# A quantised feed-forward matmul: plain tiles against Strassen's seven block products

## What is computed

```python
def _dequant(weight_q, scale, zp):          # weight_q (2048, 2048) int32, scale and zp (2048, 64)
    q = weight_q.astype(jnp.float32).reshape(N, num_groups, gs)
    return ((q - zp[:, :, None]) * scale[:, :, None]).reshape(N, K)
w = _dequant(weight_q, scale, zp)
out = jnp.einsum('bsk,nk->bsn', x, w) + bias       # x (2, 1024, 2048)
x = x + _L0_ffn_ref(_layernorm(x, axis=-1), ...)   # the layer's input is added back
```

## Time and profile before

| | |
|---|---|
| three timed runs | 2302.66, 2303.94, 2315.09 us (median 2303.94) |
| the profiled execution: time, span | 2315.36 us, 2313.6 us |
| PE busy | 2196.6 us, 95% of the span, 11560 matmuls |
| DVE, ACT, POOL busy | 57%, 46%, 43% |
| moved by DMA | 424.6 MB, mean 184 GB/s |
| granted TensorE clock, mean | 0.97 |
| gated products | about 950 to 1310 us |
| feed-forward: first and last matmul | 1598.4 and 2310.1 us |

### The profile page before, as it was taken

One profiled execution on the slowest core, in us unless ns is written; L12 is line 12 of the kernel. 1 busy time (PEld: TensorE's weight loads), 2 busy tenths in 40 slices (PEclk: granted clock), 3 DMA queues, 4 the chain that ended last, 5 costly groups with the idle time before them and its releaser, 6 DMA issues.

```text
span 2313.6 us, 34024 instructions
## 1 busy us (share of the span) xinstructions
PE 2196.6 (95%) x11560; PEld 1802.5 (78%) x11560; DVE 1325.6 (57%) x1734; ACT 1065.9 (46%) x1596; POOL 995.5 (43%) x621
## 2 busy tenths in 40 slices
PE   6898989999988999899999999998999999999999
PEld 4777766666657888788788889997778888888887
DVE  6777766777746888423332357677564364374222
ACT  3444448888875777521321356666322122122111
POOL 0111138999997677200000187873353253153110
PEclk8999989999997999899999999999999999999999
DMA  5678763333335665445453568779665565565443
GB/s 183 205 229 264 235 185 87 97 102 96 105 86 172 218 216 219 157 131 177 144 175 121 189 224 317 295 291 334 226 207 176 163 212 168 160 209 176 152 137 100
DMA packets 208916, 424.60 MB, mean 184 GB/s; under 512 B 16482, under 2 KB 132194, under 8 KB 181940
## 3 DMA queue, kind: packets, MB, share of 16 engines
q1 hardware_dynamic: 208820, 423.31, 56.2%
HBM read 284.31 MB, written 138.67 MB: 183 GB/s over the span
## 4 chain that ended last, share of the span: by engine, by line
PE 72%; DMA 9%; DVE 8%; ACT 4%; issue 4%; POOL 2%; SPq 2%; DVEq 0%; ACTq 0%; POOLq 0%
PE s_psF L2695 9%; PE s_psF L2696 9%; PE s_psF L2697 9%; PE s_m_psG L2317 7%; PE s_m_psU L2317 7%; PE s_psO L922 4%; PE s_w_psA L1901 4%; PE s_w_psB L1901 4%; DMA s_q_xc<-xP 4%; PE s_psS L868 4%; PE s_psX L899 3%; PE s_w_psR L1406 2%; DMA s_f_q<-wq 2%; DVE s_a_mx L948 1%; PE s_w_psT L1933 1%
## 5 line engine op out<-in xcount | busy, mean ns | idle before, releaser
L2695 PE MATMUL s_psF<-s_f_wh,s_f_xh 128*128 128x512 f32 x1024 | 400.2, 391 | 9.7 <-DVE s_f_xl L2573 5.0
L2697 PE MATMUL s_psF<-s_f_wh,s_f_xl 128*128 128x512 f32 x1024 | 399.1, 390 | 0.0
L1053 POOL TENSOR_TENSOR s_a_pl<-s_a_pf,s_a_ph 128x1024 fp32r<-128x1024 f32 x128 | 302.0, 2393 | 21.8 <-ACT s_a_pf L1010 21.7
L2569 ACT ACTIVATE s_f_xh<-s_f_xl 128x2048 fp32r<-128x2048 f32 x64 | 122.7, 1917 | 359.0 <-PE s_psF L2697 326.0
L2668 POOL TENSOR_TENSOR s_f_xb<-s_f_xb,s_f_fb 128x512 f32<-128x512 f32 x64 | 93.2, 1456 | 341.6 <-DMA s_f_xb<-x 324.7
L2069 POOL TENSOR_TENSOR s_w_yl<-s_w_y,s_w_yh 128x1024 fp32r<-128x1024 f32 x32 | 76.0, 2399 | 370.0 <-ACT s_w_yh L1981 370.0
L948 DVE TENSOR_REDUCE s_a_mx<-s_psS 128x1 f32<-128x512 f32 (+2 forms) x248 | 179.2, 754 | 97.0 <-PE s_psS L876 96.7
L2695 PEld LDWEIGHTS s_psF<-s_f_wh,s_f_xh 128*128 128x128 f32 x1024 | 192.7, 188 | 52.8 <-DVE s_f_xl L2573 6.7
L2697 PEld LDWEIGHTS s_psF<-s_f_wh,s_f_xl 128*128 128x128 f32 x1024 | 192.6, 188 | 40.1
L2696 PE MATMUL s_psF<-s_f_wl,s_f_xh 128*128 128x512 f32 x512 | 200.0, 391 | 0.0
L2573 DVE TENSOR_TENSOR s_f_xl<-s_f_xl,s_f_xh 128x2048 fp32r<-128x2048 f32 x64 | 160.0, 2501 | 48.5 <-ACT s_f_xh L2569 48.5
(11 more groups left out here) (316 smaller groups left out, 5633.8 us busy)
## 6 DMA issues: line engine op xcount, KB each, us to landing
s_f_xl<-xnT SPq DMA_DIRECT2D x64, 1024.0 KB, 5.8
s_q_xt<-xT SPq DMA_DIRECT2D x16, 1024.0 KB, 7.7
s_q_xc<-xP SPq DMA_DIRECT2D x16, 1024.0 KB, 9.8
hsD<-s_q_hs SPq DMA_DIRECT2D x16, 1024.0 KB, 4.9
s_w_hin<-hsD SPq DMA_DIRECT2D x16, 1024.0 KB, 5.0
hs<-s_w_res SPq DMA_DIRECT2D x16, 1024.0 KB, 3.9
s_m_raw<-giT SPq DMA_DIRECT2D x32, 512.0 KB, 4.8
mlpT<-s_m_mo SPq DMA_DIRECT2D x64, 256.0 KB, 2.4
```

Source lines behind the costliest of these rows:

```text
L1053: pool.tensor_tensor(pl[:, r, cols], pf[:, j - 1], ph[:, r, cols], ALU.subtract).then_inc(pl_ok, 1)
L2695: pe.matmul(out[:], xh[:, u % 2, kt], high(c, kt), start=(kt == 0), stop=False)
L2697: mm = pe.matmul(out[:], xl[u % 3][:, kt], high(c, kt), start=False, stop=(kt == KD - 1))
```

## The change

**The product.** Rows are cut into two halves (tiles 0 to 7, 8 to 15), the inner dimension into two, and each pair of column blocks (a group, GROUPS = 2) into its two blocks. The 2x2 by 2x2 block product is then done with seven products in place of eight; each product's factors are sums or differences of one or two blocks, and its result is added to, or subtracted from, one or two of the four blocks of the output. The table PRODUCTS lists for each product its row terms, its weight terms and its targets:

**SP's order.** Per unit u: wait for `finish(u)`, store what is complete, load the rows of unit u+4 (one or two terms), load pieces of the next product's weights (one or two terms), load a base where one is due:

```diff
+            for u in range(SEAM, UNITS):
+                sp.wait_ge(y_ok, adds[u + 1])
+                for cell in touched(u):
+                    if last_unit[cell] == u:
+                        store(sp, cell)
+                if u + 4 < UNITS:
+                    load_x(sp, u + 4)
+                    load_second(sp, u + 4)
+                for n in pieces(u):
+                    load_piece(sp, n)
```

**DVE's order** is `finish(u-1)`, `lo_x(u+2)`, then the low parts of the pieces that SP loaded at unit u-2; POOL's is `add_second(u+2)`, `add_piece` of those pieces, bias of a base:

```diff
         def vector(dve):
-            for u in range(3, UNITS):
-                for v in made_in(u):
-                    less_zero(dve, v)
-                finish(dve, u)
+            for u in range(SEAM, UNITS):
+                if u > SEAM:
+                    finish(dve, u - 1)
                 if u + 2 < UNITS:
                     lo_x(dve, u + 2)
-                for v in made_in(u):
-                    lo_piece(dve, v)
+                for n in pieces(u - 2):
+                    lo_piece(dve, n)
```

**The weights** are no longer made in the feed-forward. All four blocks are made in the gated products, 16 portions of 1 MB in place of 4, and eight differences of halves (`p_diff`, stored as `wD`) for the first product of each group:

```diff
-        made = (11, 18, 35, 42)
+        made = tuple(range(4, 4 + 3 * C * KH, 3))
...
+                if u - 5 in made:
+                    plane["difference"](dve, made.index(u - 5))
```

More of the change, by code:

```diff
@@ L2051, in body @@
                     normalise(s, p)
+                    if not live(1):
+                        between(s.off - TILES if s.reg is None else None)
                     evacuate(s, 0)
@@ new lines, in store, with product, touched @@
+            sp.dma_start(dst, w[:, i % RING]).then_inc(w_out, 16)
+            if second(i):
+                sp.wait_ge(diff_ok, pairs(i) + 1)
+                dst = io["wD"][i // (2 * KH)].rearrange("p (r j n) -> p r j n", j=KH, r=KH // 2)[:, :, i % KH]
+                sp.dma_start(dst, diff[:]).then_inc(d_out, 16)
+        return dict(load=load, less_zero=less_zero, times_scale=times_scale, difference=difference, store=store,
+                    w_out=w_out, d_out=d_out, groups=C * KH)
+def build_ffn(nc, io, k, zone, w2):
+    PAIRS = TILES // 2
+    HK = KD // 2
+    GROUPS = C // 2
+    PRODUCTS = (
[7 more added lines that the diff above has]
+    )
+    STEPS = len(PRODUCTS)
+    UNITS = GROUPS * STEPS * PAIRS
+    SEAM = PAIRS
+    ISSUE = (0, 0, 1, 2, 3, 4, 5, 6)
+    def product(u):
+        return PRODUCTS[u // PAIRS % STEPS]
+    def touched(u):
+        return [(u // (STEPS * PAIRS), half, n, u % PAIRS) for half, n, _ in product(u)[3]]
+    adds, last_add, first_add, last_unit = [0], {}, set(), {}
+    for u in range(UNITS):
+        adds.append(adds[-1] + len(product(u)[3]))
+        for cell in touched(u):
+            last_unit[cell] = u
+    two = [0]
+    for u in range(UNITS):
+        two.append(two[-1] + (len(product(u)[1]) == 2))
+    made = [0]
+    for n in range(UNITS):
+        made.append(made[-1] + (len(product(n)[2]) == 2))
+    summed_x = [u for u in range(UNITS) if two[u + 1] > two[u]]
+    summed_w = [n for n in range(UNITS) if made[n + 1] > made[n]]
+    stores = {}
+    for u in range(UNITS):
+        for cell in touched(u):
+            if last_unit[cell] == u:
+                stores[cell] = len(stores)
+    base_at = {}
+    for j in range(PAIRS):
+        base_at[0, 0, 1, j] = base_at[0, 1, 1, j] = j - 2 * PAIRS
+        base_at[0, 0, 0, j] = j + 4
+        base_at[0, 1, 0, j] = j + 14
+        for half, n in ((0, 1), (1, 0), (0, 0), (1, 1)):
+            base_at[1, half, n, j] = last_unit[0, half, n, j] + (4 if (half, n) == (0, 1) else 2)
+    bases = sorted(base_at, key=lambda cell: (base_at[cell], cell[1]))
+    base_of = {cell: b for b, cell in enumerate(bases)}
+    RB, RY, RW = 8, 4, 5
@@ new lines, in build_ffn, with acc, high, low @@
+        mm_ok, b_ok, y_ok, fb_in = (sem(n) for n in ("mm_ok", "b_ok", "y_ok", "fb_in"))
+        def acc(cell):
+            return home[cell[1:]]
+        def high(q, kt):
+            if q % 2:
+                return wh1[:, kt]
+            return whA[:, kt] if kt < 2 else whB[:, kt - 2]
+        def low(q, kt):
+            if q % 2:
+                return wl1[:, kt]
+            return wlA[:, kt] if kt < 2 else wlB[:, kt - 2]
+        def rows(u, term):
+            half, part, _ = term
+            return io["xnT"][u % PAIRS + PAIRS * half][:, part * HK * P:(part + 1) * HK * P]
@@ new lines, in weights, with load_second @@
+        def weights(q, term, kt):
+            part, n, _ = term
+            at = (part * HK + kt) * H
+            return io["wF"][q // STEPS * 2 + n][:, at:at + H]
+        def load_x(sp, u):
+            if u >= 4:
+                sp.wait_ge(mm_ok, u - 3)
+            sp.dma_start(xl[u % 4][:].bitcast(F32).rearrange("p t j -> p (t j)"), rows(u, product(u)[1][0])).then_inc(x_in[u % 4], 16)
+        def load_second(sp, u):
+            if len(product(u)[1]) == 2:
+                i = two[u]
+                if i >= 3:
+                    sp.wait_ge(x_lo, summed_x[i - 3] + 1)
+                sp.dma_start(xs[i % 3][:].rearrange("p t j -> p (t j)"), rows(u, product(u)[1][1])).then_inc(xs_in[i % 3], 16)
@@ new lines, in store, with pieces @@
+        def store(sp, cell):
+            g, half, n, j = cell
+            i, tile, c = stores[cell], half * PAIRS + j, 2 * g + n
+            if i >= RY:
+                sp.wait_ge(y_out[i % RY], 16 * (i // RY))
+            sp.dma_start(io["y"][tile * P:(tile + 1) * P, c * H:(c + 1) * H], acc(cell)[:]).then_inc(y_out[i % RY], 16)
+        def pieces(u):
+            q, m = (u + 1) // PAIRS + 1, (u + 1) % PAIRS
+            if q >= GROUPS * STEPS:
+                return ()
+            return tuple(q * HK + kt for kt in range(HK) if ISSUE[kt] == m)
@@ L2604, in times_scale @@
[L2604 to L2614 removed]
+            load_x(sp, 11)
+            load_second(sp, 11)
@@ new lines, in sync, with whole_x, whole_w @@
+            for r in range(RY):
+                sp.wait_ge(y_out[r], 16 * len(stores) // RY)
+        def whole_x(u):
+            return xs[two[u] % 3][:] if len(product(u)[1]) == 2 else xl[u % 4][:].bitcast(F32)
+        def whole_w(n):
+            if made[n + 1] > made[n]:
+                return ws[:, made[n] % 4]
+            return low(n // HK, n % HK).bitcast(F32)
+        def hi_x(act, u):
+            if len(product(u)[1]) == 2:
+                act.wait_ge(x_sum, two[u] + 1)
+            else:
+                act.wait_ge(x_in[u % 4], 16 * (u // 4 + 1))
+            if u >= 3:
+                act.wait_ge(mm_ok, u - 2)
+            act.activation(xh[u % 3][:], whole_x(u), ACT.Copy).then_inc(x_hi, 1)
```

471 lines of the change are left out of this document (273 added, 198 removed).

## The result

The changed kernel takes **2406.1 us** (median of 4 runs, 2404.8 to 2409.9). Beside it the kernel before took 2309.5 us, a ratio of **1.042** (95% interval 1.038 to 1.046): 4.2% slower, where the forecast was 0.7% faster and its range ended at 2338. The profiled execution spans 2404.4 us, 90.8 more than that of before.

What follows compares the result with a forecast made beforehand. The prediction took the feed-forward as bound by PE's number of matmuls. Its terms, -87 - 5 + 59 + 12 + 5 = -16 us, put the median of 2303.9 us at 2288 us, 0.7% faster, range 2240 to 2338.

Steps and rivals of the forecast that it cites:

- Step 1: Feed-forward on PE: 3072 matmuls become 2688 at an unchanged 0.2267 us each, -87.0 us.
- Step 2: Feed-forward: PE's waits where weights are made from integer pieces go away, -5 us.
- Step 3: Feed-forward: the loop through SP's loads takes 6.27 us per unit against PE's 5.44, +59 us including turns.
- Rival B: Feed-forward loop is longer, rows landing in 6.7 us: term +106, 2335 us in all; chance 0.28.
- turns of POOL and DVE over the bias: Feed-forward, first group: a bias add standing between costs 0.6 us per unit in some 25 units, 15 us.
- Step 4: Gated products: added weight portions cost only where rows and second-half weights load together, +12 us (+2 to +25).
- Rival C: Gated products: 3 MB bursts delay rows in all chunks, costing 45 us instead of 12, 2321 us; chance 0.10.
- Step 5: Joint before the feed-forward: earlier first pieces give -4, late rows and lost slack cost more, +5 us (-4 to +15).
- Rival A: Feed-forward: the loop does not bind, turns alone do, costing 16 us; 2245 us in all; chance 0.22.

Runs made afterwards that it cites:

- a1_order: Changed kernel with the feed-forward's loads of rows and weight pieces issued before SP's wait for the additions: 2312.7 us, 1.002 of the kernel before.
- p1_plane: Kernel before with all sixteen weight portions and eight differences made in the gated products, its feed-forward untouched: 2352.2 us, ratio 1.019.
- a3_align: Changed kernel with most feed-forward weight tiles moved up 576 bytes, onto a multiple of 2,048: 2402.0 us, 1.040 of the kernel before.
- a4_128: Changed kernel with the same weight tiles as a3_align moved up only 64 bytes, onto a multiple of 128: 2397.4 us in one run.
- c1_order_align: Changed kernel with the edits of a1_order and a3_align together: 2307.4 us, 0.999 of the kernel before.
- b1_bias: c1_order_align with portions' stores a unit earlier and the feed-forward's bias additions from the eighteenth on moved from POOL to DVE: 2304.2 us, ratio 0.997.
- p4_rows: p1_plane with ACT's rounding and DVE's subtraction of next-chunk rows one unit later in the gated products: 2317.1 us, 1.002 of the kernel before.

## Why the prediction was wrong, step by step

The joint and feed-forward split up by the runs: the matmuls alone were 3072 x 0.2267 = 696.4 us and are 2688 x 0.2333 = 627.1; a1_order is the changed kernel without the loop.

| step | forecast | measured | how |
|---|---|---|---|
| 1, matmuls | -87 | **-69.3** | 627.1 - 696.4 |
| 3, loop | +59 | **+89.8** | 773.5 - 683.7 |
| 2, 5 and the rest: weight making, joint, turns, transfers | -5 + 5 | **+32.6** | (683.7 - 627.1) - (720.4 - 696.4) = 56.6 - 24.0; not one cause |
| 4, portions | +12 | **+44.7** | 404.0 - 359.3; p1_plane +42.6 |

- **Step 1** took the step of a matmul from the old placement as a constant. The count was right, and the step is one that the diff decides: an offset of 7616 in `build_ffn` cost 0.0066 us x 2688 = 18 us of matmul time, of which 9 to 13 showed in the stretch (a3_align, a4_128, c1_order_align). I read this line and did not ask what an address could do.
- **Step 2** wasn't measured by itself: nothing in the feed-forward makes weights from integers any more, and what that gave is inside the 32.6.
- **Step 3** had the right mechanism, chain and place, and the landing mis-sized. Term by term the round above measured 0.38 to issue (forecast 0.39), **6.67 to land (5.5)**, 2.4 (2.35), 1.1 (1.06), 1.15 (1.23), 0.6 (0.6), 1.3 (1.3): 13.6 against 12.4 (the text's 12.5 is its own terms rounded up). Rival B had this landing, gave it 0.28 and priced the loop at +106, where +90 was measured. The text itself called 6.7 "as near as 5.8" and then took 5.5, below the nearest row for loads in a calmer stage, for a stage in which a unit moves 2 MB in 5.44 us where that one moved 1.5 MB in 10.88. That the pieces form a second chain was missed, but cost nothing in the sum, since both close at nearly the same time. Of the 59, 15 were for turns of POOL and DVE over the bias; those no run shows: with the bias off POOL (b1_bias) nothing came back. So the loop proper was put at 44 (56 less 12 of slack) and took 90.
- **The rule of the Trainium skill** that I set beside it ("DMA: Bandwidth & Descriptors", section "Anatomy of one DMA") is a fit for DMAs issued from GpSimd, and gives an estimate of 2.0 us + 524,288 / 436e3 = 3.2 us for one such row block; the median landing was 5.2 for the first and 6.4 for the second. The row was the better guide, and still too low.
- **Step 4** failed twice. At the place that it priced, rows and second-half weights beside the bursts of units 25 and 28, the loss was 26.6 us instead of 12 (from the first matmuls of the units: 17.0 in units 28 to 30, 9.6 in unit 32), over its own upper bound of 25. And it called the rest free because bytes over time were below what the engines can move, where four more groups of eight units lost 18 (3.0, 4.4, 3.9 and 6.7). ACT rounds a row block in the unit in which it is issued, so any landing longer than about a unit stops the gate. The 28 row loads of the stage landed in 6.5 us in the median (4.7 before), 12.2 at most, and ACT's longest wait, 17.6, holds 5.6 us more in which the load wasn't issued yet. The price was Rival C's, 45; its reason against, that rows are loaded a chunk ahead, was false of the queue: they are loaded a chunk ahead and waited for at once. p4_rows, with 35 of 43 us back, shows it.
- **Step 5**: PE reached its first matmul 5.8 us after the write's last (9.1 before), as the -4 said. Then the first product took 7.9 us per unit (8.2 in a1_order). Of the 32.6 us about 8 are there (8 units and the start lose 26.4 us in a1_order against 18.0 before), nearly all the rest in the second, third, sixth and seventh product of the first group (7.1, 6.8, 6.2 and 5.9 us per unit in a1_order). Rival A put 16 us there for turns; the place was right, but b1_bias shows that POOL's turns are not the only bound. What holds these products stays open.
- **The sum.** All the large misses have one sign. They are not independent: steps 3 and 4 each took a stage with more traffic at the price of one with less. With the forecast's own mechanism and the landing of Rival B, the price of C, and 18 us for the step, it would have been -87 - 5 + 106 + 45 + 5 + 18 = +82, near the 90.8 of the profiled executions, partly by luck: its 106 is 16 over the loop as measured, which stands in for half of the 32.6 that nobody forecast. Cases B and C were near one by one and were given chances as if only one of them could be true.

## What to carry to other kernels

When an edit halves the work of a step and keeps its bytes, price every transfer at the landing of the busiest stage of the trace, and look in every in-order queue for who stands behind the instruction that waits for it; free average bandwidth says nothing about that. A load that only needs a buffer should be issued when the buffer is free, not behind a wait for a result: here that line decided 94 us of 2406. And before trusting fewer matmuls at the same step, see that the moved operand tiles keep their alignment.
